# Transposing sums spread by a table, with more pairs of products added on GpSimd and VectorE

## The reference

```python
h = einsum('bchw,oc->bohw', xk, reduce_w) + reduce_b
kern = einsum('bchw,oc->bohw', h, span_w) + span_b      # 16 groups x 49 taps per place
out = (kern * patches).sum(axis=3)                      # sum over the 49 taps
...
topk_probs, topk_idx = top_k(softmax(flat @ router_w.T), 2)
h = silu(h1) * h3                                       # hidden size 341
y = einsum('neh,ech->nec', h, w2)
```

## Time and profile before

| | us |
|---|---|
| median of 3 runs | 1515.86 |
| lowest, highest | 1513.18, 1517.63 |
| the profiled execution | 1514.45 |
| its span, first to last instruction | 1512.6 |

### The profile page before, as it was taken

One profiled execution on the slowest core, in us unless ns is written; L12 is line 12 of the kernel. 1 busy time (PEld: TensorE's weight loads), 2 busy tenths in 40 slices (PEclk: granted clock), 3 DMA queues, 4 the chain that ended last, 5 costly groups with the idle time before them and its releaser, 6 DMA issues.

```text
span 1512.6 us, 25000 instructions
## 1 busy us (share of the span) xinstructions
PE 1300.8 (86%) x8596; PEld 1127.5 (75%) x8596; DVE 1074.7 (71%) x2247; ACT 415.9 (27%) x1055; POOL 830.7 (55%) x573
## 2 busy tenths in 40 slices
PE   0598988899999999999999999999999999848871
PEld 0387777788888888888888878888788888737661
DVE  2599899887877878778777887778878778422220
ACT  2112020322323223232232323323232131423330
POOL 1233535357475564756647566475664747464454
PEclk9999999999999999999999999999999999988996
DMA  5001010333334343333433434334333333456662
GB/s 145 13 1 37 20 43 23 88 74 99 74 88 94 74 101 73 86 94 76 99 78 82 96 74 98 79 81 102 67 87 85 83 81 78 108 116 149 147 132 36
DMA packets 91230, 123.37 MB, mean 82 GB/s; under 512 B 13042, under 2 KB 68466, under 8 KB 91104
## 3 DMA queue, kind: packets, MB, share of 16 engines
q1 hardware_dynamic: 54592, 94.95, 21.9%
q0 software_dynamic: 36512, 26.83, 13.0%
HBM read 87.17 MB, written 34.56 MB: 80 GB/s over the span
## 4 chain that ended last, share of the span: by engine, by line
PE 60%; DVE 14%; issue 8%; DMA 7%; ACT 6%; POOL 3%; SPq 1%; POOLq 0%; DVEq 0%; ACTq 0%
PE acc_ps L390 22%; PE kern_ps L468 15%; DVE prod L853 8%; PE bank L500 7%; DMA out<-y_sb,xs 5%; PE hid_ps L492 5%; PE hid_ps L491 5%; PE bank L390 3%; DVE stats_ln L723 3%; POOL out L983 3%; PE bank L421 2%; PE bank L448 1%; ACT L632 1%; DVE x_res L860 1%; ACT rows L583 1%
## 5 line engine op out<-in xcount | busy, mean ns | idle before, releaser
L853 DVE TENSOR_TENSOR prod<-kern_ps,xn 128x896 f32<-128x896 f32 x686 | 733.2, 1084 | 77.8 <-PE kern_ps L468 72.0
L468 PE MATMUL kern_ps<-h_stack,span 98*128 98x448 f32 x1372 | 477.1, 431 | 85.0 <-DVE prod L853 82.7
L390 PE MATMUL acc_ps<-consts_sb,prod 128*128 128x128 f32 x3920 | 545.7, 276 | 0.0
L983 POOL DMA_INDIRECT out<-y_sb,xs x210 | 330.2, 1572 | 335.3 <-ACT y_sb L645 245.1
L390 PEld LDWEIGHTS acc_ps<-consts_sb,prod 128*128 128x128 f32 x3920 | 471.6, 143 | 51.9 <-issue 12.0
L992 POOL TENSOR_TENSOR prod<-prod 128x896 f32<-128x896 f32 x126 | 270.3, 2146 | 183.5 <-DVE prod L853 182.5
L468 PEld LDWEIGHTS kern_ps<-h_stack,span 98*128 98x128 f32 x1372 | 227.9, 194 | 136.8 <-DVE prod L853 120.1
L971 POOL DMA_INDIRECT sorted_x<-rows,dst x196 | 190.7, 973 | 68.3 <-issue 53.7
L632 ACT ACTIVATE silu<-hid_ps 114x256 f32<-114x256 f32 x228 | 87.3, 383 | 418.4 <-PE hid_ps L492 418.2
L873 DVE TENSOR_TENSOR hid<-hid_ps,silu 114x256 f32<-114x256 f32 x228 | 96.2, 422 | 103.0 <-ACT silu L632 102.9
L491 PE MATMUL hid_ps<-xc,w_sb 128*114 128x256 f32 x456 | 137.5, 383 | 1.3
(11 more groups left out here) (93 smaller groups left out, 939.2 us busy)
## 6 DMA issues: line engine op xcount, KB each, us to landing
w_sb<-in_w SPq DMA_DIRECT2D x105, 342.0 KB
w_sb<-in_w SPq DMA_DIRECT2D x105, 192.0 KB, 2.4
xs<-sorted_x SPq DMA_DIRECT2D x105, 130.0 KB, 2.1
x_ln<-in_x SPq DMA_DIRECT2D x14, 448.0 KB, 3.8
x_res<-in_x SPq DMA_DIRECT2D x14, 448.0 KB, 3.5
out<-x_res SPq DMA_DIRECT2D x14, 448.0 KB, 2.5
out<-y_sb,xs POOLq DMA_INDIRECT x210
sorted_x<-rows,dst POOLq DMA_INDIRECT x196, 2.4
```

The source lines that it names most:

```text
L390: return mm(dst, lhsT=src, rhs=eye, is_transpose=True, start=start, stop=True, skip_group_check=True)
L468: i = mm(kern_ps[:, n % 2, h, 0:HALF], span[:, u * C:(u + 1) * C], h_stack[:, m % 2, h * HALF:(h + 1) * HALF], start=True, stop=True)
L853: v.tensor_tensor(tiled(prod[:, n % PRING, :].rearrange("p (h n) -> p h n", h=2)), tiled(kern_ps[:, n % 2, :, 0:HALF]), window(m, u // KS, ...
L983: g.indirect_dma_start(out[:, :], bass.IndirectOffsetOnAxis(ap=xs[:, j % XBUFS, b, C:C + 1].bitcast(U32), axis=0), y_sb[:, j % YBUFS, b, : ...
```

## The change

**Items.** All twelve groups have their pair (4g, 4g+1) added by GpSimd. In groups 1, 4, 7 and 10, and only in tiles with experts beside them (3 to 13), VectorE adds the second pair (4g+2, 4g+3) itself, directly behind the product of tap 4g+3, that is at taps 7, 19, 31 and 43. Tiles 0 to 2 have 37 items, 259 transposes; the others 33 items, 231 transposes. The ring has 10 buffers.

**Table.** The number of blocks of each slot is now written in two tables of 49 numbers, one for tiles with experts beside them, one for those without.

**Two conversions move to ScalarE.** `dst` is written there in slot 26 (`places`), `weight_i` in slot 30 (`weight_rows`). For the last tile `places` stands behind expert tile `BESIDE` + 5. The last tile's `weight_i` stays on VectorE. The clamp of `weight_i` is left out in the moved one.

```diff
-PAIRED = (0, 1, 2, 4, 5, 6, 8, 9, 10)
-PRING = 9
+POOL_PAIRS = tuple(range(12))
+DVE_PAIRS = (1, 4, 7, 10)
+PRING = 10
...
         u = 4 * g
-        if g in PAIRED:
-            items += [(u + 2, None, u + 3), (u + 3, None, u + 4), (u, u + 1, u + 5)]
+        if g in DVE_PAIRS and beside_experts(m):
+            items.append((u + 2, u + 3, u + 4))
         else:
-            items += [(u + i, None, u + i + 1) for i in range(4)]
+            items += [(u + 2, None, u + 3), (u + 3, None, u + 4)]
+        items.append((u, u + 1, min(u + 6, TAPS)))
...
+BLOCKS_BESIDE = (14, 0, 0, 7, 7, 0, 0, 0, 8, 1, 12, 3, 6, 0, 0, 0, 2, 10, 0, 2, 7, 12, 0, 8, 6, 5, 8, 0, 0,
+                8, 0, 4, 13, 8, 0, 0, 1, 9, 0, 0, 9, 12, 0, 0, 8, 13, 9, 11, 8)
...
-        while todo and len(now) < (SUM_BLOCKS[n % CYCLE] if 1 < n % TAPS < TAPS - 2 else 11) and todo[0][0] <= n:
+        m, u = divmod(n, TAPS)
+        most = (BLOCKS_BESIDE if beside_experts(m) else BLOCKS_ALONE)[u] if m < TILES else len(todo)
+        while todo and len(now) < most and todo[0][0] <= n:
...
+            def places(m):
+                act.wait_ge(s_rt, RT * m + 15)
+                act_f(dst[:, m % 2], dst_f[:], ACT.Copy).then_inc(s_dst, 1)
...
+                    if u == 26:
+                        places(m - 1)
+                    if u == 30 and m - 1 >= 1:
+                        weight_rows(m - 1)
...
+                if i == 5:
+                    places(last)
...
-                elif k == 15:
-                    i = v.tensor_copy(dst[:, m % 2], dst_f[:])
...
+            def add_pair(n):
+                a = prod[:, (n - 1) % PRING, :]
+                dve.wait_ge(s_prod, n + 1)
+                v.tensor_tensor(a, a, prod[:, n % PRING, :], ALU.add).then_inc(s_dpair, 1)
...
                 if n >= 0:
                     product(n)
+                    if any(u == it[1] for it in DVE_ITEMS[m]):
+                        add_pair(n)
...
-                    pool.wait_ge(s_rt, RT * m + 16)
+                    pool.wait_ge(s_rt, RT * m + 12)
+                    pool.wait_ge(s_dst, m + 1)
```

More of the change, by code:

```diff
@@ L113, with freed_by @@
 SUMS = sum_schedule()
-def item_of(u):
-    for i, (a, b, _) in enumerate(ITEMS):
-        if a == u:
-            return i
-    return None
+def freed_by(n):
+    m, u = divmod(n, TAPS)
+    for i, (a, b, _) in enumerate(ITEMS[m]):
+        if u == a:
+            return m, i, False
+        if u == b:
+            return m, i, True
 SHARED = ((11, "xn2_0", -1), (15, "xn2_1", -1), (17, "logits", -1), (24, "rank", -1),
@@ L473, in sums @@
                 for m, i, b in SUMS[n]:
-                    tap, second, _ = ITEMS[i]
+                    item = ITEMS[m][i]
+                    tap, second, _ = item
                     if i == 0 and b in (0, 4) and m:
@@ L845, in product @@
                 if n >= PRING:
-                    r, w = divmod(n - PRING, TAPS)
-                    item = item_of(w)
-                    if item is None:
-                        pair = next(i for i, it in enumerate(PAIRS) if it[1] == w)
-                        dve.wait_ge(s_pair, r * len(PAIRS) + pair + 1)
+                    r, i, added = freed_by(n - PRING)
+                    item = ITEMS[r][i]
+                    if not added:
+                        dve.wait_ge(s_sum, sum(len(x) + 1 for x in ITEMS[:r]) + i + (2 if i == len(ITEMS[r]) - 1 else 1))
+                    elif item in POOL_ITEMS[r]:
+                        dve.wait_ge(s_pair, count_before(POOL_ITEMS, r) + POOL_ITEMS[r].index(item) + 1)
                     else:
-                        dve.wait_ge(s_sum, r * (len(ITEMS) + 1) + item + (2 if item == len(ITEMS) - 1 else 1))
+                        dve.wait_ge(s_dpair, count_before(DVE_ITEMS, r) + DVE_ITEMS[r].index(item) + 1)
                 v.tensor_tensor(tiled(prod[:, n % PRING, :].rearrange("p (h n) -> p h n", h=2)),
                                 tiled(kern_ps[:, n % 2, :, 0:HALF]), window(m, u // KS, u % KS), ALU.mult).then_inc(s_prod, 1)
+            def add_pair(n):
+                a = prod[:, (n - 1) % PRING, :]
+                dve.wait_ge(s_prod, n + 1)
+                v.tensor_tensor(a, a, prod[:, n % PRING, :], ALU.add).then_inc(s_dpair, 1)
             def evict(m):
@@ L937, in _ @@
                     if i == 4:
-                        for k in ((12, 13, 14), (15, 16, 17, 18), ())[c]:
+                        for k in ((12, 13, 14), (15, 16, 17), ())[c]:
                             router_step(last, k)
@@ L988, in _ @@
                 m, u = divmod(n, TAPS)
-                if 0 <= m and u % 4 == 2 and (u - 2) // 4 in PAIRED:
+                if 0 <= m and any(u == it[1] + 1 for it in POOL_ITEMS[m]):
                     a = prod[:, (n - 2) % PRING, :]
```

56 lines of the change are left out of this document (38 added, 18 removed).

## The result

| | before | after |
|---|---|---|
| median, us | 1514.56 (4 runs) | 1527.31 (4 runs) |
| lowest, highest | 1513.18, 1517.63 | 1525.61, 1528.45 |
| span of the profiled execution | 1512.6 | 1523.8 |
| mean granted TensorE clock over the span | 0.969 | 0.952 |

The ratio is 1.008, with a 95% interval of [1.006, 1.010]: the change makes the kernel slower, by 12.8 us, a small difference but one clear of the noise. The forecast was 1473 us, faster, with a range that ended at 1499.

A forecast was written before the change was run, and what follows sets the result against it. TensorE and VectorE were taken to hand the limit to each other within a tile. Eleven tiles -41, tiles 0 to 2 -7 and the tail +5.4 gave -42.6 us, forecast 1473 us, 8-in-10 range 1452 to 1499.

The forecast's parts named there:

- the adds on VectorE: Taps 7, 19, 31 and 43 of tiles 3 to 13: 1.12 us of VectorE each, 4.5 us per tile.
- a dip in about every second tile: TensorE's clock in middle tiles: the forecast is wrong if it dips more often than in every second tile.
- The ring: Seven pairs have their sum one slot ahead of the product taking their buffer, which must wait for those transposes.
- 2.2 us of waits: Taps 13 to 33 of tile 6: waits left after following the tap starts, giving 41.0 us, 3.4 gained.
- line 833's removal: VectorE's second small conversion: its removal gives nothing, as the next instruction, line 834, waits for the same GpSimd pair.
- slower rival: VectorE's adds wait for GpSimd pairs, up to 2.1 us each: +2.5 us in eleven tiles, 1542 us; chance 0.06.
- The rule weighed against the change: On VectorE, a CAST and operations with two SBUF operands, including every new add, wait for a GpSimd pair.
- The CAST's 2.0 us per tile: Line 788's conversion of dst on VectorE, stalled by a GpSimd pair: moving it to ScalarE saves VectorE 2.0 us.
- tiles 0 to 2: Tiles without experts: gains of 4, 2 and 1 us for tiles 1, 2 and 0, 7 us together.
- GpSimd in time at tap 46: From tap 36, GpSimd needs 21.2 us until its new pair ends; transposes need it 24 us after: nothing added.
- the tail: After the last product: ScalarE writes the last tile's places later, delaying sends and the last stage's load by 5.4 us.
- A middle tile at 90.2: Tile length in the new profile: near 90.2 us, with PE busy near 83.9 of it.

The follow-up runs named there:

- hid_first: The changed kernel with VectorE's add moved behind the hidden product of the same tap instead of ahead of it: 1490.40 us, ratio 0.985 to the kernel before.
- hid19: The changed kernel with the add moved behind the hidden product at tap 19 alone: 1499.02 us, ratio 0.989 to the kernel before.
- ring12: The changed kernel with 12 ring buffers instead of 10 (PRING): 1509.74 us, ratio 0.996 to the kernel before.
- casts_only: The kernel before with only the two conversions (dst and weight_i) moved to ScalarE: 1485.20 us, ratio 0.981 to the kernel before.
- hid_ring_tail: The changed kernel with adds behind the hidden products, 12 ring buffers and the last tile's dst on VectorE: 1471.75 us, ratio 0.973 to the kernel before.
- best_steps: hid_ring_tail with VectorE's small table steps moved to other taps, away from GpSimd's pairs: 1465.88 us, ratio 0.967 to the kernel before.

## Why the prediction was wrong

**The step that failed: the adds on VectorE.** They were priced at 1.12 us of VectorE time each, and that price was right (1.09 at the median). What the step left out is who stands behind them. The prediction shows the order at tap 19, product, add, hidden product, and never asks who waits for the hidden product. TensorE does, with the down matmuls next in its order. The add shifts them by 1 us in a place where TensorE has just been idle 1.08 us. In the prediction's sum this delay stands at nothing. hid_first, which changes this and nothing else, took 37 us off; hid19 put 28 of them on that one tap.

**The clock.** The forecast counted a dip in about every second tile as before, and named more dips as what would make it wrong. There were 15 instead of 5. Tiles 10 and 11 show what they cost: 2.8 us in a tile with two dips that has the same work as one with none, so some 1.4 us for each, and ten more of them some 14 us. The five of tap 27 went with the CAST. Of the 15 that came eight stand at tap 20, behind the add, and none of them is left in hid19 or hid_first. That the second idle stretch brings the dip is what the two orders show: with it ten of eleven tiles have a dip at tap 20, without it none. It does not always do so: tile 11 of after and seven of eleven tiles of ring12 have a second idle stretch and no dip, and what decides there stays open. The dips at tap 3 were not followed up; casts_only has three of them without any add, so they do not hang on the adds alone.

**The ring.** It was seen ("seven sums now stand one slot ahead"), but within "2.2 us of waits" for taps 13 to 33, and followed in one stretch only. Its full price was 5.3 us of VectorE's waiting in tile 6, and 17.6 us of time against after (ring12), 12.2 once the dips are gone (hid_ring_tail). Of the 5.3 us, 2.9 (0.48 at tap 38 and 2.38 at tap 42) lie in taps 34 to 48, where the sum had no wait for the ring: 24.3 was measured there for 23.8.

**The stalls behind pairs.** Of line 833's removal the text said that it gives nothing since the next instruction waits instead. In casts_only that was so. In the whole change it became more: 24.4 us in the three instructions of steps 12 and 13 (13.4 on line 833, 2.0 on 834, 9.0 on 837; sums over 13 tiles) became 33.4 (6.0 on line 881, 27.4 on line 884), and past_step rose from 2.8 to 19.4. Together 26 us more of VectorE's time in these steps, what the CAST had cost (26.0). This was priced at 2 us once in tile 2, and at nothing for tap 30 elsewhere. At tap 30 of after, 2.76 us stand where 1.39 stood; at tap 33, 4.19 for 3.65. That best_steps still found 5.9 us shows that this is a real term.

**What held.** The mechanism of the slower rival did not come true in after, though its sign did: only 2 of the 44 adds overlapped a pair, by 0.52 and 0.97 us, since the others stand a tap behind its start. The kernel came out slower for a reason that the rival did not name. The rule weighed against the change, that GpSimd contends with DVE instructions with two SBUF inputs (the Trainium skill, GPSIMD Engine Reference, section Key points), is borne out, but by the small steps: `past_step` 199 ns at its shortest and 1594 at the median, `done` 168 and 2748. For the 896-wide add it is borne out by the two of after, 1.48 and 1.93 us, and by 22 of the 44 in best_steps, 1.52 to 2.37. The CAST's 2.0 us per tile, ScalarE's copy (0.25 taken, 0.206 measured), tiles 0 to 2 (7 forecast, 8.8 measured), the adds, GpSimd in time at tap 46 (TensorE waits nowhere in after for a pair), and the tail (5.4 forecast, 4.8 measured; the idle of PE forecast near 29, 29.63 measured) held. A middle tile at 90.2 was forecast, and hid_ring_tail has 90.50. Its time of 1471.75 is not proof of every term, though: it lacks the tail's 5.4 that the forecast contained, so that on equal terms the forecast was some 4 to 5 us too low, about what best_steps recovers. That its number is within 2 us of the forecast is in part luck.

**How the 54 us add up.** The measured time is 54 us above the forecast. The hidden product behind the add makes 37 of them (about half of it waits, half the clock) and the ring 12. The other 5 are what the forecast was too low on equal terms; the stalls of the table steps are the likely term, since best_steps took 5.9 off by moving them, but no run shows that it is this one alone. The effects are not independent: the ring is worth 17.6 where the dips are present, 12.2 where they are not.

## What to carry over

An instruction put into an in-order queue costs its own time on that queue and a delay for everything behind it: for each, ask which engine has the consumer of the next instruction at the head of its own queue, and put the new work behind that instruction, not before. When several changes come as one, time the small ones alone; here two small conversions held 29 us, nearly all of it in one of them, more than the rest. And a buffer whose sum stands one slot ahead of its reuse has no slack: count every such place over the whole tile before saving a buffer.
